# Spreading the choice of experts over the four tiles of a chunk in a fused state-space and mixture-of-experts kernel

## The reference

```python
logits = x @ router_w;  scores = sigmoid(logits)                 # 32 experts in 8 groups of 4
group_scores = top_k(scores_grouped, 2).sum(-1)
_, top_groups = top_k(group_scores, 4);  masked = scores outside them set to 0
_, top_k_index = top_k(masked, 8);  tkw = 2.5 * scores[top_k_index] / their sum
# rows are sorted by expert; routed = sum of tkw * down(silu(gate(x)) * up(x)) per token
shared = silu(x @ sw_gate) * (x @ sw_up) @ sw_down
return x + ssm_branch(x) + routed + shared
```

## Time and profile before

| | |
|---|---|
| median of 3 runs | 11932.23 us (11924.78 to 11934.33) |
| the profiled execution's own time | 11944.92 us |
| its span, first to last instruction | 11943.2 us |
| mean granted TensorE clock | 0.985 of full speed |
| PE busy | 11556.5 us, 97% |
| DVE busy | 4983.5 us, 42% |
| POOL busy | 4264.7 us, 36% |

### The profile page before, as it was taken

The page is one execution under the profiler, slowest core; times in us unless marked ns, Lnnn a source line. Parts: engine busy times, 40 slices in busy tenths (PEclk is TensorE's granted clock), DMA queues, the critical chain, the costliest instruction groups (busy, mean ns, idle before and its releaser), DMA issues.

```text
span 11943.2 us, 201881 instructions
## 1 busy us (share of the span) xinstructions
PE 11556.5 (97%) x52608; PEld 9490.3 (79%) x52609; DVE 4983.5 (42%) x6765; ACT 2405.2 (20%) x3041; POOL 4264.7 (36%) x4233
## 2 busy tenths in 40 slices
PE   8999779998999999999999999999999999999998
PEld 7777557776888888888888888888887788888887
DVE  5656566664333333333433343333434434333332
ACT  2111144442111111111211121121212212111111
POOL 2555442222333333333333333333333333333332
PEclk9999889999999999999999999999999999999999
DMA  4333266765333333333433343343445434333332
GB/s 157 124 126 126 91 174 174 180 177 152 61 80 66 84 64 85 83 87 80 106 63 82 63 119 71 62 104 63 104 98 142 108 64 124 63 64 85 62 61 56
DMA packets 728560, 1174.21 MB, mean 98 GB/s; under 512 B 462930, under 2 KB 463122, under 8 KB 705400
## 3 DMA queue, kind: packets, MB, share of 16 engines
q0 software_dynamic: 212608, 622.54, 24.4%
q1 hardware_dynamic: 486136, 443.39, 11.9%
q10 hardware_dynamic: 29696, 106.96, 3.6%
HBM read 714.72 MB, written 457.73 MB: 98 GB/s over the span
## 4 chain that ended last, share of the span: by engine, by line
PE 72%; issue 1%; DVE 1%; DMA 0%; DVEq 0%; ACT 0%; SPq 0%; POOL 0%; ACTq 0%; POOLq 0%
PE pg L66 8%; PE pg L68 8%; PE pg L67 8%; PE pd L68 8%; PE pd L66 8%; PE pd L67 8%; PE pu L67 8%; PE pu L66 8%; PE pu L68 8%; PE ta L1970 2%; DVE w_lo L1868 0%; DVEq L1591 0%; DMA xq<-xn_rows,idx_q 0%; ACT w_hi L1801 0%; DMA quads<-slot_table 0%
## 5 line engine op out<-in xcount | busy, mean ns | idle before, releaser
L1762 POOL DMA_INDIRECT out_rows<-y,idx_s x528 | 859.9, 1629 | 4637.5 <-issue 4620.2
L1754 POOL DMA_INDIRECT xq<-xn_rows,idx_q x2120 | 2165.6, 1021 | 935.5 <-issue 485.5
L66 PE MATMUL pg<-w_hi,x_hi 128*128 128x512 f32 x4224 | 1699.9, 402 | 46.7 <-DVE x_lo L1884 40.3
L66 PE MATMUL pd<-w_hi,a_hi 128*128 128x512 f32 x4224 | 1645.2, 389 | 10.2 <-DVEq L1909 10.2
L68 PE MATMUL pg<-w_hi,x_lo 128*128 128x512 f32 x4224 | 1651.9, 391 | 0.0
L67 PE MATMUL pg<-w_lo,x_hi 128*128 128x512 f32 x4224 | 1646.9, 390 | 0.0
L68 PE MATMUL pd<-w_hi,a_lo 128*128 128x512 f32 x4224 | 1646.0, 390 | 0.0
L67 PE MATMUL pd<-w_lo,a_hi 128*128 128x512 f32 x4224 | 1644.2, 389 | 0.0
L66 PE MATMUL pu<-w_hi,x_hi 128*128 128x512 f32 x4224 | 1643.1, 389 | 0.0
L67 PE MATMUL pu<-w_lo,x_hi 128*128 128x512 f32 x4224 | 1643.1, 389 | 0.0
L68 PE MATMUL pu<-w_hi,x_lo 128*128 128x512 f32 x4224 | 1643.1, 389 | 0.0
(11 more groups left out here) (289 smaller groups left out, 15197.7 us busy)
## 6 DMA issues: line engine op xcount, KB each, us to landing
stage<-in_w_all SPq DMA_DIRECT2D x174, 1024.0 KB
rep<-steps ACTq DMA_DIRECT2D x192, 512.0 KB
quads<-slot_table SPq DMA_DIRECT2D x2120, 1.0 KB
xq<-xn_rows,idx_q POOLq DMA_INDIRECT x2120
xt<-in_x SPq DMA_DIRECT2D x64, 512.0 KB
xn_rows<-xn SPq DMA_DIRECT2D x64, 512.0 KB, 2.6
xn_turned<-sx_hi SPq DMA_DIRECT2D x64, 512.0 KB
xn_turned<-sx_lo SPq DMA_DIRECT2D x64, 512.0 KB
```

What stands on the lines that cost most here:

```text
L66: m(dst, hi, whi[:, cols], start=begin, stop=False)
L1754: g.indirect_dma_start(out=xq[q][:, n], out_offset=None, in_=xn_q, in_offset=bass.IndirectOffsetOnAxis(ap=idx_q[q][:, n:n + 1], axis=0))\
L1762: g.indirect_dma_start(out=out, out_offset=bass.IndirectOffsetOnAxis(ap=idx_s[q][:, 0:1], axis=0), in_=y[q][:], in_offset=None, compute_op ...
```

## The change

`route` gets five parts in place of four. The old part 1 is cut behind the search for the eight experts (`i8`): what follows, the one-hot rows `oh`, their sum `sel` and `prod`, becomes part 2, and the old parts 2 and 3 become 3 and 4. Then the parts are placed anew: part 0 and the short part 1 in the tile with k = 1, part 2 in k = 2, part 3 in k = 3, and the part that was 3 and is 4 stays alone in k = 0 of the chunk after. With part 0 a tile later, `z` is ready a tile later: PE turns it in k = 2 in place of k = 1, ACT copies it in k = 3 in place of k = 2, and SP stores it at the end of k = 3, behind two other stores.

```diff
@@ SP @@
-                    if k == 3 and not known(c, 0):
-                        store_z(c - 1, 1 - r)
                     if not ends(c, k, 1):
                         store_turned(*later(c, k, 1))
                     if not (known(c, 0) and k == 0):
                         store_out(*later(c, k, -1))
+                    if k == 3 and not known(c, 0):
+                        store_z(c - 1, 1 - r)
@@ ACT @@
-                    if k == 2 and not known(c, 0):
+                    if k == 3 and not known(c, 0):
                         z_row(c - 1, 1 - r)
@@ PE @@
-                    if k == 1 and not known(c, 0):
+                    if k == 2 and not known(c, 0):
                         z_turned(c - 1)
@@ DVE @@
-                s = Steps(dve, rt_step, c * RT + (0, 7, 17, 21)[part], dve_passed)
+                s = Steps(dve, rt_step, c * RT + (0, 7, 14, 17, 21)[part], dve_passed)
...
                     s(last)
+                    assert s.n == 7, s.n
+                if part == 2:
                     s(v.tensor_copy(i8f[:], i8[:]))
...
-                if part == 2:
+                if part == 3:
...
-                if part == 3:
+                if part == 4:
...
-                        route(c - 2, r, 3)
-                    if k < 3 and not known(c, 0):
-                        route(c - 1, 1 - r, k)
+                        route(c - 2, r, 4)
+                    if k and not known(c, 0):
+                        for part in ((0, 1), (2,), (3,))[k - 1]:
+                            route(c - 1, 1 - r, part)
```

## The result

Changed kernel: median 11906.99 us of 21 runs (11899.18 to 11917.17). Kernel before, beside it: 11924.78 us of 21 runs (11912.29 to 11941.01). Ratio 0.9983, 95% interval 0.9976 to 0.999: 17.8 us faster. The forecast, 11863 us, lay 69 us under the median of three runs that it started from, and 62 us under this one. The profiled execution took 11907.07 us with a span of 11905.5, on its median; the profiled one of before had 11944.92 us, 20 above its own. So the profiles differ by 37.7 us, and only they show where.

A forecast was written before the change was run, and what follows sets the result against it. PE bounds `route_stage`, so its standing time can be won: 53.7 (waits) + 10 (uncounted) + 13.6 (clock) - 6.5 (`gif`) - 1.4 (stage's end) = 69.4 us, from 11932.2 to 11863 us. Range 11848 to 11907.

The forecast's parts named there:

- What the copy `gif` may cost there: Tile after k = 1: POOL's add may hold this copy, a wait of 0 to 0.8 us; 6.5 us lost in all.
- Waits removed: `route_stage`: PE's waits for DVE's `ssg` and `sa_lo` all go in the four tiles, 53.7 us won.
- The threshold: PE waits for as long as `sa_lo` starts later than about 7.9 us after PE's last transposes `ta`.
- The clock: Half-clock stretches behind the two waits of k = 1, in eight of 13 chunks, should go: 13.6 us won.
- Moves at no cost: Later `z` on PE, ACT and SP, and `ranks` needing `sel`, cost nothing; ACT's lost cover would cost 8 us.
- The stage's end: Behind the last chunk, the k = 3 part stands in front of `sa_lo`: 1.4 us later.
- the 79.5 us named as a sign: Length of a chunk expected in the profile after, if the forecast holds: about 79.5 us.
- the 10 us for what waits don't show: Each of 38 PE waits costs some 0.3 us beyond its shown length: 10 us won, bounds 0 and 15.
- B: Rival, 0.09: POOL's add holds `gif` the whole 2.4 us and a 2.2 us step follows the search; about 11906 us.
- C: Rival, 0.06: a loop from `ssg` over POOL's scatters and add to `sa_hi`, `sa_lo` sets the pace; 11903 us.
- D: Rival, 0.07: nothing moves, since `sa_hi` comes late by itself and DVE isn't waited for; 11932 us.
- E: Rival, 0.03, the slower one: denser matmuls lower the granted clock; at 0.88 55 us slower, 11987 us.

The follow-up runs named there:

- g2: Changed kernel with POOL's add moved ahead of its eight scatters and the ranks' 14 matmuls written as 8: 11834.36 us, ratio 0.9971.
- e2: Changed kernel with POOL's add moved ahead of its eight scatters: 11880.70 us, ratio 0.996.
- h1: Changed kernel with only the ranks' 14 matmuls written as 8, POOL's add left behind the scatters: 11862.04 us, ratio 0.9996.
- e3: Kernel before with POOL's add moved ahead of its eight scatters, nothing else: 11866.36 us, ratio 0.9949.
- f7: Changed kernel with POOL's add ahead of the scatters and SP's z stores back in front: 11882.32 us, ratio 0.9951.
- g1: Changed kernel with POOL's add ahead of the scatters and the ranks' 14 matmuls issued three times over: 11880.89 us, ratio 1.001.
- f5: Kernel before with POOL's add ahead of the scatters and only the z path of the change: 11879.58 us, ratio 0.995.
- f6: Kernel before with POOL's add ahead of the scatters and only the piece `w8` to `payload` moved to k = 3: 11878.22 us, ratio 0.9949.
- g3: Kernel before with POOL's add ahead of the scatters and the ranks' 14 matmuls issued three times over: 11884.70 us, ratio 1.0014.
- i1: Changed kernel with the ranks' 14 matmuls written as 8, on a chip where `sa_hi` is late: 11885.89 us, ratio 0.9963.
- i2: Kernel before with POOL's add ahead of the scatters, again, on the fifth chip, where `sa_hi` is late: 11862.65 us, ratio 0.9942.
- h4: Kernel before with POOL's add ahead of the scatters and the ranks in 8 matmuls, on the fourth chip: 11835.12 us, ratio 0.9974.
- g4: Kernel before with POOL's add ahead of the scatters and the ranks in 8 matmuls, on the third chip: 11833.47 us, ratio 0.997.
- h2: Kernel before with only the ranks' 14 matmuls written as 8: 11864.29 us, ratio 0.9999.
- h3: Changed kernel run again unedited on the fourth chip, where `sa_hi` isn't late: 11866.86 us, ratio 1.0001.

## Why the prediction was wrong

The sign was right and the size was not: 69.4 us forecast against 37.7 us between the profiles and 17.8 us between the medians.

**The failed step is "What the copy `gif` may cost there": 0.5 us in each of 13 chunks, 6.5 us in all.** The step priced one copy, asked whether POOL's add would meet it, and bounded the whole by the wait that such a meeting gives. In the chunk shown the add began 1.9 us after `ta`, near the 2.4 us forecast, so ahead of `gif`, and met part 0, whose instructions with two inputs in SBUF are held like a copy. Its bound for `sa_lo`, 8.7 us, was under the 9.2 us measured; over 9 us was what the prediction had named as a sign of being wrong. The mean over the chunks is 9.0 us in the changed kernel and, with the add first and nothing late (g2), 6.3 us: the working up to there was right. Held, the tile after k = 1 has 22.31 us; with the add first, 20.38 us (e2, another chip): 1.9 us by 13 chunks are 25 us where 6.5 stood. Where nothing is late it is 21.90 (h1) against 19.95 us (g2), 25 us again; the times of these two, on two chips with before at 11866 and 11868 us, are 28 us apart.

The Trainium skill, page "SBUF — State Buffer", section "Who interferes with whom", names the two-input instructions beside the copy; the prediction quoted it, and then priced the copy alone. The earlier trace rows show a held copy, and nothing there said that the rest was safe. The page also has the one that comes second blocked, and the prediction let the trace agree. As recorded it doesn't quite: `i8f` starts at 588.97 and the add at 589.61, and in the profile of after the held instructions start up to 0.6 us ahead of the add (654.28 and 654.85). Spans on POOL are rough, so which came first isn't shown; that the held one ends 0.05 to 0.3 us after the add is.

**Waits removed** (53.7 us): right for the tiles after k = 0, 2 and 3, which have none. The threshold holds within 0.2 us for the tile after k = 1 as well. DVE waits for `rstd` behind `sa_lo`, 0.97 us in every chunk of before and in every second one of after: there `sa_lo` at 9.22 us gave a wait of 1.53 us, a threshold of 7.7. In the others that wait is 1.32 us, and 9.17 us gave 1.83. So 19.5 us of the 53.7 stayed, where the forecast let them all go and put 6.5 back.

**The clock** (13.6 us): eight half-level stretches became four, so about half was won. That it hangs on PE's standing is borne out: no stretch is left in the loop of e2 and e3, where 2.6 and 2.9 us of waits are left; f7, with 9.6 us of waits, has one, and g1 one behind each gap.

**"Moves at no cost"**: true of `z` and of SP's stores, as far as a measurement goes (f5: 0.995 against 0.9949 for f6). What no step had is the growth of PE's gaps of issue from 4.0 to 10.4 us in 12 chunks, 7 us of the stage. They grow with the length of the burst of short matmuls, by g1 and g3, and i1 fits. Why before's layout shows fewer than the others isn't settled; f5 and f6, one edit each from it, have them, but on another chip.

**The stage's end** (1.4 us): from the last `ta` (1409.2; 1369.2) to the scan's first product 50.5 us became 51.5: right.

**The sum.** Its terms for the loop give 53.7 + 10 + 13.6 - 6.5 = 70.8 us in 13 chunks, 5.4 each, so 80.3 us a chunk from 85.7; the 79.5 us named as a sign is 0.8 us lower than the prediction's own terms give. The 1.6 us by which the add of k = 1 ends ahead of `ta` are those of k = 0; its own rows give 585.19 - 583.26 = 1.9. That changes nothing above: unheld, `sa_lo` came at 6.3 us.

So of the 31.7 us missing between the profiles, some 18.5 are the mis-sized step, with the clock's four stretches in it, and 7 the gaps. The other 6 aren't told apart; the 10 us for what waits don't show, too, was only an estimate. The further 20 us down to the medians is the profiled execution of before, which lay above its median; one trace can't say where that time was.

**The rivals.** B gave 11906 us, and the time came out at 11907, the top of the range. That is in part luck: B had `sa_lo` at 10.9 us, where it came at 9.0 to 9.2, and 26 us of gain, where the profiles show 37.7 and the medians 17.8. Its rule (POOL's add costs each chunk the whole 2.4 us) was right (2.0 to 2.9 us over an instruction's own length in part 0), its detail was not: `gif` was held once only, and no late step stood behind the search for `i`. C, a loop from POOL's add over `sa_hi`, falls: where nothing is late `sa_hi` starts 1.9 us ahead of the add (482.80 and 484.71), and the changed kernel has the same long tile. D's cause, `sa_hi` late by itself, is real but not what PE waits for in the changed kernel: `sa_lo` starts 9.0 us after `ta` with it and without it. It decides what the kernel before costs, and so what there is to win. E didn't occur.

**The best version** that the runs point to is the kernel before with the add first, 64 and 67 us faster than before where `sa_hi` is late (e3, i2); with the short ranks it is 31 and 34 us faster where it isn't (h4, g4), 2 of them by the short ranks alone (h2). The spread adds nothing to it: 11834 against 11833 us (g2, g4). Both edits together weren't run where `sa_hi` is late.

## What to carry to other kernels

When a piece of work is moved beside a long POOL instruction, put every DVE instruction of that piece with two SBUF inputs, and every copy, on the list of what can be held, and ask where the long instruction can go instead: moving the one add was worth 64 us on a chip where the whole change brought some 18 on its own, and about 30 where the change brought none. A piece that is long by its stall (here 13.5 us with 5.1 of stall) is mended at the stall first. Try the halves of a change apart: here the half without part 0's move gained at least as much as the whole. And measure on more than one chip before a change of 0.2% is called a gain.

## What the runs showed of the hardware

- **ACT can begin late what PE has released, on some chips.** With POOL's scatters under way, ACT began `sa_hi` by up to 5.2 to 6.9 us after `ta` in the profiles of before and after and all ten on three chips; in eight profiles on two other chips by 0.04 us, the changed kernel among them on both kinds. Without scatters (the first two chunks of the profile of after) it is at once: `ta` ends at 104.33, `sa_hi` starts at 104.36 us. The profile calls such waits "remote", ended by an update whose sender it doesn't show. That the scatters are the cause isn't shown, since no run leaves them out, nor whether the signal or the instruction comes late. On the two chips the kernel before takes 11866 and 11868 us, on the three 11930 to 11938. What on a chip makes it so is not known.
- **DVE's own step can be late as well**: in three chunks of e2 `gif` waited 1.7 to 2.2 us ("remote") behind the search for `gi`. Above it waited 2.15 us, and started at 486.24, where ACT's `sa_hi`, due since `ta` at 480.71, started at 486.26. Both came free together.
- **Short matmuls are paid for later.** 42 matmuls of 128 x 32 in 1.2 us were followed by 3.6 to 4.3 us in which PE issued nothing, at the loop's jump back (g1; 4.6 to 5.1 us in g3); 14 by 0.3 to 1.5 us in most chunks of the changed kernel where `sa_hi` is late (by less in before's) and by none where it isn't; 8 by 0.4 us at most. In the last chunk, straight code behind the loop, PE's single matmuls of 0.37 us come at 0.7, 1.4 or 2.1 us steps for some 15 to 20 us on the chips where `sa_hi` is late. That PE's instructions are brought to it too slowly is argued from this, not shown.
- **One held instruction waits out the add, however short it is**: a minimum of 128 x 32 takes 3.03 us instead of 0.18, one of the four `scalar_tensor_tensor` of `z` up to 3.1 us instead of 0.31, in the changed kernel on a chip with late `sa_hi` and on one without (h3).
